# Trailing the weighted sums by six slots instead of seven in a fused decoder layer

## The reference, cut to what matters

```
x = x + fast_weights(layernorm(x))            # 16 heads, sequences of 8 blocks
x = x + cross_attention(layernorm(x), ctx)    # the stage that is changed
x = x + routed_experts(layernorm(x))          # 8 experts, top 1, capacity 256

# cross_attention: 8 heads of 128, 2048 queries against 2048 keys
sim  = einsum('hid,hjd->hij', q, k) * SCALE
sim  = (sim - mean) * 1.5 + mean              # softmax is blind to the mean
attn = softmax(sim)
out  = einsum('hij,hjd->hid', attn, v)
y    = out @ Wout + bout
```

## Time and profile before

| what | value |
|---|---|
| median of 3 runs | 1412.86 us (1411.82 to 1415.68) |
| profiled execution | 1415.48 us, span 1413.8 us |
| PE / DVE / ACT / POOL busy | 94% / 79% / 64% / 63% of the span |
| granted TensorE clock, mean | 0.982 |
| attention slots, first to last score | 445 to 1240 us |

### The profile page before, as it was taken

One profiled execution on the slowest core, in us unless ns is written; L12 is line 12 of the kernel. 1 busy time (PEld: TensorE's weight loads), 2 busy tenths in 40 slices (PEclk: granted clock), 3 DMA queues, 4 the chain that ended last, 5 costly groups with the idle time before them and its releaser, 6 DMA issues.

```text
span 1413.8 us, 20498 instructions
## 1 busy us (share of the span) xinstructions
PE 1330.0 (94%) x7244; PEld 1090.7 (77%) x7244; DVE 1116.2 (79%) x1711; ACT 901.6 (64%) x1325; POOL 885.3 (63%) x535
## 2 busy tenths in 40 slices
PE   5999999988999899999999999999999999994998
PEld 4788887876788677777777777777777777773997
DVE  6799998947712779989898988989898998985454
ACT  4544434124655587877777777877778777676674
POOL 2201012124331199998999989989989989874453
PEclk9999999999999999999999999999999999997999
DMA  7502023124565588887888878878878878786572
GB/s 225 80 3 68 1 67 90 33 59 168 201 197 212 161 230 210 208 208 196 211 209 192 220 188 204 219 189 211 206 194 213 211 175 211 178 223 242 180 249 77
DMA packets 171970, 241.22 MB, mean 171 GB/s; under 512 B 34035, under 2 KB 77429, under 8 KB 171872
## 3 DMA queue, kind: packets, MB, share of 16 engines
q1 hardware_dynamic: 156720, 210.21, 58.2%
q10 hardware_dynamic: 13104, 23.86, 5.0%
q0 software_dynamic: 2048, 5.90, 1.1%
HBM read 64.79 MB, written 41.32 MB: 75 GB/s over the span
## 4 chain that ended last, share of the span: by engine, by line
PE 51%; DVE 15%; ACT 5%; issue 4%; DMA 1%; POOL 0%; SPq 0%; ACTq 0%; DVEq 0%; POOLq 0%
PE xa_S L1486 20%; PE xa_O L1503 12%; DVE xa_mxp L1279 5%; PE xa_Y L1440 5%; PE xa_Y L1515 4%; PE ex_H L1938 3%; PE ex_Y L1950 3%; ACT xa_probs L1659 3%; PE xa_O L1440 3%; DVE xa_tq L1292 3%; DVE xa_mx_nb_rinv L1277 2%; DVE hall L1313 2%; DVE xa_mx_nb_rinv L1282 1%; DMA xa_moved<-xa_tq 0%; DVE xa_mx_nb_rinv L1308 0%
## 5 line engine op out<-in xcount | busy, mean ns | idle before, releaser
L1162 POOL TENSOR_TENSOR xa_pT<-xa_moved,xa_pT 128x1024 fp32r<-128x1024 f32 x246 | 586.2, 2406 | 35.8 <-ACT xa_pT L1653 32.6
L1486 PE MATMUL xa_S<-xa_kT,xa_qT 128*128 128x512 f32 x1536 | 397.6, 408 | 14.7 <-ACT xa_probs L1659 11.0
L1659 ACT ACTIVATE xa_probs<-xa_S,xa_mx_nb_rinv 128x1024 f32<-128x1024 f32 x256 | 286.2, 1118 | 174.7 <-DVE xa_mx_nb_rinv L1282 174.6
L1503 PE MATMUL xa_O<-xa_pT,xa_v 128*128 128x512 f32 x1536 | 376.2, 394 | 2.6 <-DVE xa_pT L1335 2.6
L1486 PEld LDWEIGHTS xa_S<-xa_kT,xa_qT 128*128 128x128 f32 x1536 | 286.1, 190 | 102.6 <-ACT xa_probs L1659 41.4
L1503 PEld LDWEIGHTS xa_O<-xa_pT,xa_v 128*128 128x128 f32 x1536 | 289.0, 188 | 68.7 <-DVE xa_pT L1335 2.9
L1292 DVE STREAM_TRANSPOSE xa_tq<-xa_probs 128x1024 f32<-128x1024 f32 x256 | 316.8, 1238 | 13.7 <-ACT xa_probs L1659 6.0
L1653 ACT ACTIVATE xa_pT<-xa_moved 128x1024 fp32r<-128x1024 f32 x254 | 254.1, 1050 | 3.9 <-DMA xa_moved<-xa_tq 3.7
L1277 DVE TENSOR_REDUCE xa_mx_nb_rinv<-xa_S 128x1 f32<-128x1024 f32 x128 | 155.6, 1216 | 80.0 <-PE xa_S L1486 77.7
L1279 DVE TENSOR_REDUCE xa_mxp<-xa_S 128x1 f32<-128x1024 f32 x128 | 157.5, 1231 | 17.8 <-PE xa_S L1486 17.8
L473 PE MATMUL fw_pp<-fw_hT,fw_wqk 128*128 128x512 f32 x384 | 97.9, 405 | 7.4 <-DVE fw_hT L612 4.5
(11 more groups left out here) (228 smaller groups left out, 1811.0 us busy)
## 6 DMA issues: line engine op xcount, KB each, us to landing
xa_moved<-xa_tq SPq DMA_DIRECT2D x508, 256.0 KB, 4.5
heads_k<-ci_outs SPq DMA_DIRECT2D x32, 256.0 KB, 2.0
heads_v<-ci_outs SPq DMA_DIRECT2D x32, 256.0 KB, 2.3
heads_q<-ci_outs SPq DMA_DIRECT2D x32, 256.0 KB, 2.2
xa_chunk<-heads_v ACTq DMA_DIRECT2D x32, 256.0 KB, 3.7
ex_w1s<-in_L_ffn_w_dram SPq DMA_DIRECT2D x8, 1024.0 KB, 7.0
ex_w2s<-in_L_ffn_w_dram SPq DMA_DIRECT2D x8, 1024.0 KB, 9.5
xa_chunk<-heads_q ACTq DMA_DIRECT2D x31, 256.0 KB, 3.5
```

What stands on the lines that cost most here:

```text
L1162: pool.tensor_tensor(quadrants(pT[LO], r), unit_moved(r), quadrants(pT[HI], r).bitcast(F32), ALU.subtract).then_inc(lo_ready, 1)
L1486: last = pe.matmul(S[:, k], qT[a][:, i // GT % 2, q], kT[b][h % 2][:, k * 512:(k + 1) * 512], start=(n == 0), stop=(n == 2))
L1503: last = pe.matmul(O[:], v[a][:, j * P:(j + 1) * P], pT[b][:, r % PRING, k], start=(j == 0 and n == 0), stop=(j == JT - 1 and n == 2))
L1659: act.activation(probs[:, unit % RING], S[:, 2 * u:2 * u + 2].rearrange("p a b -> p (a b)"), ACT.Exp, bias=nb[:, s % 2:s % 2 + 1], scale=S ...
```

## The change

`LAG` goes from 7 to 6, and every entry of the drain's table that stood a slot after `SLOTS + 1` comes one slot earlier; END as well. `LAST`, the slots of the output projections and sums, and the slots of `copy_oT`, `high_part` and `low_part` follow from LAG. What stays where it was: scores, maxima, exponentials, transposes, the moves' condition on them, and the slots of the chunks.

```diff
-LAG = 7
+LAG = 6
...
-        END = SLOTS + 14
-        OUTPUTS = {(30, 0): 3, (30, 1): 3, (31, 0): 7, (31, 1): 7}
-        SUMS = {(30, 0): 3, (30, 1): 4, (31, 0): 7, (31, 1): 7}
-        ROUTING = {"transposes": (0, 2, 4, 8), "copies": (0, 2, 4, 8), "logits": (1, 3, 5, 9), "choose": (2, 3, 5, 9),
-                   "positions": (3, 4, 6, 10), "place": (3, 4, 6, 11),
-                   "statistics": (None, None, 4, 8), "root": (1, 1, 4, 8), "scale": (1, 2, 4, 9), "rows": (1, 2, 5, 9),
-                   "exp": (3, 3, 5, 10)}
+        END = SLOTS + 13
+        OUTPUTS = {(30, 0): 2, (30, 1): 2, (31, 0): 6, (31, 1): 6}
+        SUMS = {(30, 0): 2, (30, 1): 3, (31, 0): 6, (31, 1): 6}
+        ROUTING = {"transposes": (0, 1, 3, 7), "copies": (0, 1, 3, 7), "logits": (0, 2, 4, 8), "choose": (1, 2, 4, 8),
+                   "positions": (2, 3, 5, 9), "place": (2, 3, 5, 10),
+                   "statistics": (None, None, 3, 7), "root": (0, 0, 3, 7), "scale": (0, 1, 3, 8), "rows": (0, 1, 4, 8),
+                   "exp": (2, 2, 4, 9)}
```

## The result

| | median | runs | scores of slot 7 start | scores of slot 127 start | a group, slots 7 to 127 | from there to the end |
|---|---|---|---|---|---|---|
| before, lag 7 | 1414.12 us | 4 (1411.82 to 1415.68) | 495.79 | 1236.96 | 24.71 us | 176.8 us |
| after, lag 6 | 1452.71 us | 4 (1450.97 to 1455.63) | 503.34 | 1276.34 | 25.77 us | 176.0 us |

The ratio is 1.0278 (95% interval 1.026 to 1.0297): slower by 38.6 us, where 34 were forecast. The profiled execution has a span of 1452.3 us. Most of the loss is in the beat: (1276.34 - 503.34) / 30 = 25.77 us a group, 1.06 us more than the 24.71 us before by the same count, or 32 us in 30 groups. (An undisturbed group took 24.64 us before; against that it is 1.13 us.) Some 7 us more are the head: from the scores of slot 0 to those of slot 7 it takes 57.4 us instead of 50.4.

A forecast was written before the change was run, and what follows sets the result against it. A loop through PE, DVE and ACT bounds the kernel; at lag 6 a move's landing enters it. Slot 127 33.4 us later (27 from the groups) and drain +1 give +34 us: 1449.9 profiled, 1447 us median, range 1428 to 1473.

The forecast's parts named there:

- The bound and its place: ACT's high part of move 4g, line 1653, waits for its landing: some 30 waits, 60 to 90 us in all.
- The terms of the cycle: Scores to three slots on: 8.11 + 0.4 + 7.5 + 1.91 + 1.26 = 19.2 us, against 18.33 before.
- issue to last landing: Four DMAs of move 4g, first issue to last landing: 7.5 us taken, nearly all groups read 7.0 to 8.1.
- crowding: Move 4g+1 issued at once behind move 4g, as in the head; the group's 0.85 us taken as 0.9.
- Head: Start of attention: high_part(0) delays slot 5's exponential, scores fall one slot behind; slot 7 at 503.17, where slot 8 was.
- Drain: After the last scores: one slot less but no sooner landing; +1 us, bounds -6 and +3.
- move 124: In the drain, ACT's wait for this move's landing sets the time; it comes no sooner, rather 1 to 2 us later.
- The value chunks: PE waits for POOL's low parts up to 0.9 us a head, covered by ACT's wait; uncovered 7 us at most.
- The clock: Rival: PE's clock falls after the new idle gap of about 1.1 us, 30 x 1.5 us more; 1493 us, chance 0.04.
- The sum: Whole kernel: slot 127 starts 33.4 us later, drain 1 us longer; in all +34 us.
- the Trainium skill's fit: Move of 1 MB estimated at 4.4 us, fitting the 5.78 us available; nothing lost in the steady part.
- The moves land as slowly as in the head: Rival in the beat: 2.0 us lost a group, +67 us, 1480 us; chance 0.17.

The follow-up runs named there:

- e2: Lag 6 kernel with move 4g of groups 1 to 30 issuing only two of its four DMAs, result not the reference's; 1420.89 us, 1.0049 of before.
- e1: Lag 6 kernel with the first half of the transposes ahead of the sum in each group's last slot; 1428.55 us, 1.0107 of before.
- e5: Lag 6 kernel with all four moves of a group waiting for the second half of its last slot's transposes; 1614.81 us, 1.1425 of before.
- e6: Kernel before (lag 7) with all four moves of a group waiting for its last slot's second transposes half; 1412.14 us, 0.9996 of before.
- e9: Lag 6 kernel with the third and fourth DMA of move 4g issued by ACT instead of SP; 1463.68 us, 1.0353 of before.
- e7: Kernel before (lag 7) with the first two moves issued ahead of the last three stores of the projections; 1413.31 us, 1.0001 of before.
- e3: Lag 6 kernel with value chunks in slots 4 to 7, query and key chunks reordered; 1453.78 us, 1.0279 of before.

## Why the prediction was right

**The bound and its place.** Shown. The wait stands where it was put, at line 1653, once in each of the 30 groups, 66.2 us of the 84.8 (some 30 idle times of 2 to 3 us, 60 to 90 us in all, were forecast). e2 takes half of the bytes away and the beat is the old one; e1 takes 0.9 us out elsewhere in the same cycle and 0.8 come back; e5 and e6 put some 4 us in, which cost time at six slots and none at seven.

**The terms of the cycle.**

| term | forecast | measured after |
|---|---|---|
| scores to end of transposes | 8.11 us | 8.11 |
| to the first issue | 0.4 | 0.03, mean of 30 groups |
| issue to last landing | 7.5, 0.05 added for crowding | 8.07, mean of 30 groups (7.16 to 9.62) |
| high parts | 1.91 | 1.91 (701.89 to 703.80) |
| exponential to PE | 1.26 | 1.24 |
| a group longer by | 0.9 | 1.13 than the undisturbed 24.64, 1.06 than the mean of 24.71 |

The mis-sized term is the landing: forecast 0.5 us too short, made good in part, by luck, by an issue 0.4 us sooner than I took. I had put 0.05 us on move 4g+1 being issued at once behind move 4g, as in the head. It does follow sooner (1.8 us behind the last issue, against 3.0 before), and in e9 four DMAs at once slow each other: the last lands after 6.9 us in the mean instead of 5.5. But this crowding is not shown to be the cause, and it can't be all of it. In e5 and e6 the two moves follow each other as closely (1.8 us in both), and the landing took 7.67 and 7.61 us there, hardly more than the 7.56 before. Within the changed kernel, the seven groups in which move 4g+1 came 2.1 to 2.4 us behind landed after 7.75 us, the others after 8.17. So the spacing may explain a part; what makes the rest of the half us stays open.

**Head.** Forecast 503.17 for slot 7, measured 503.34, of a run whose slot 0 was 0.5 us later. The size holds (e2: 7 us left); its reason was only half right (e7).

**Drain.** Forecast 1 us longer, measured 0.8 shorter. That it hangs on move 124 holds: the landing ended that wait again, 2.1 us later after the scores than before. The work behind it made up for more than that: 159.4 us from this high part to the end instead of 162.3.

**What was costed at nothing.** The value chunks do make PE wait, and it costs nothing (e3), as argued. The clock: 1.00 granted over 505 to 1235 us as a whole; at a gap of 1.73 us no fall, in one slot behind 2.77 us a fall. PE's matmul busy time is 1333.9 us against 1330.0.

**The sum.** 34 us forecast, 38.6 measured. In the profiled runs slot 127 starts 39.4 us later (33.4 forecast), and from there to the end it takes 0.8 us less (1 more). The 6 us between are in the beat: 25.77 us a group where the forecast came to 25.57. By the table the longer landing, less the sooner issue and the 0.05 us that I had added, accounts for 0.15 of these 0.20 us; the rest isn't assigned.

**The rivals.** By the Trainium skill's fit for one transfer issued from GpSimd (DMA: Bandwidth & Descriptors, Anatomy of one DMA) the estimate for a move of 1 MB was 4.4 us, which would have left the beat alone. Four DMAs of 256 KB issued by SP took 8.07 us here, and even two of them took 5.1 (e2); the measurement decides. "The moves land as slowly as in the head" was closer than I held: 8.07 lies midway between the 7.5 of the forecast and the 8.7 of the head.

## What to carry to other kernels

A lag between pipeline stages is worth what the slowest hand-over inside it needs, and it is a step: with a slot too many one pays a slot of drain (6.7 us here, 8.6 in all), with one too few the shortfall comes back in every group (1.1 us, 30 times). Before cutting it, add up from the trace, for the one hand-over with the least room, the end of the producer, the issue, the last landing and what the consumer has queued behind it, and compare with the consumer's idle time. Where it is short, look for work in front of the producer that can go behind it (e1: 24 us for a turned order) before touching the transfer.

## What the runs showed of the hardware

- Four DMAs of 256 KB from SBUF to SBUF, issued by SP one behind the other, took 7.2 to 9.6 us from the first issue to the last landing in the changed kernel (7.0 to 8.6 in the kernel before), the last alone 4.6 to 7.1; two took 4.9 to 5.5 (e2). With all four issued within 0.6 us the last landed only 0.5 us sooner (e9).
- Two DMAs of this kind took 2.3 us of ACT's sequencer (589 and 1689 ns; e9), and its high parts stood idle for issues 28 times, 90.6 us in all. On SP the four of a move took 4.1 us in the mean of the changed kernel, with the last starting 2.5 us behind the first.
- TensorE's granted clock in the changed kernel was 1.00 over 505 to 1235 us as a whole, and scores behind an idle time of 1.73 us took the full clock's 3.06 us; it was 0.66 in the 4.5 us behind idle times of 2.77 us (changed kernel) and 4.61 us (e5). The length of the idle time alone doesn't decide it: in e9 the scores behind 2.16 us took 4.54 us, at a granted clock of 0.63, and those behind 2.38 us took 3.06.
